# Twelve token tiles instead of eight gathered inside the expert loops, with eight x buffers instead of four

## The reference

```python
x = x + 0.5 * ffn(layernorm(x), ...)
x = x + attn(layernorm(x), ...)
x = x + 0.5 * ffn(layernorm(x), ...)

# ffn: 16 experts, top 4 per token, hidden width 176, and one shared expert
scores = sigmoid(logits) + gate_b
weights, indices = top_k(scores, 4); weights = weights / weights.sum(-1)
shared_out = silu(x @ w1_shared) * (x @ w3_shared) @ w2_shared
h3 = silu((x @ w1_routed[e]) * (x @ w3_routed[e]))
routed_out = sum over the 4 chosen e of weights[e] * (h3 @ w2_routed[e])
return shared_out + routed_out

# attn: xp = x W_in; dt = softplus(xp W_dt + b_dt); a = exp(-dt * exp(log_A))
# ys[t] = a[t] * ys[t-1] + xp[t]; y = ys W_out
```

## Time and profile before

| | |
|---|---|
| median of 3 runs | 588.59 us (586.60 to 590.25) |
| profiled execution | 588.09 us, span 586.1 us |
| mean granted TensorE clock | 0.912 |
| busy: PE, DVE, ACT, POOL | 83%, 75%, 64%, 60% of the span |
| x gathers (L562) | 158, 0.945 us each on POOL |
| early row gathers (L576) | 64, about 1.01 us each on POOL |
| late row gathers (L597) | 64, 0.978 us each on POOL |

### The profile page before, as it was taken

How to read it: one execution, slowest core, us unless ns; L and a number is a source line. 1 busy time by engine, 2 the same in 40 slices (tenths; PEclk the granted TensorE clock), 3 DMA queues, 4 the chain that set the end, 5 groups by cost and what they waited for, 6 DMA issues and landing times.

```text
span 586.1 us, 13303 instructions
## 1 busy us (share of the span) xinstructions
PE 486.1 (83%) x3206; PEld 448.6 (77%) x3207; DVE 437.3 (75%) x1467; ACT 372.2 (64%) x1128; POOL 353.3 (60%) x364
## 2 busy tenths in 40 slices
PE   3968789999999999687677942699999999998760
PEld 2856569999999999566565921499999999987650
DVE  6889838878888888638987589476778888867355
ACT  2687737777777777667675563477777777766100
POOL 3699754447777775477603252554467777755775
PEclk9989559999999999999997975599999999999975
DMA  8992044656656556443201460245455555674655
GB/s 283 394 350 91 27 136 109 170 163 201 200 163 169 162 165 151 132 122 107 72 2 55 144 215 1 63 115 158 135 160 159 160 173 159 157 153 136 193 165 152
DMA packets 61149, 88.25 MB, mean 151 GB/s; under 512 B 9499, under 2 KB 46363, under 8 KB 61107
## 3 DMA queue, kind: packets, MB, share of 16 engines
q0 software_dynamic: 13728, 37.50, 25.9%
q1 hardware_dynamic: 47379, 50.29, 25.0%
HBM read 57.22 MB, written 30.54 MB: 150 GB/s over the span
## 4 chain that ended last, share of the span: by engine, by line
PE 59%; DVE 12%; DMA 8%; ACT 8%; issue 6%; POOL 6%; SPq 0%; POOLq 0%; ACTq 0%; DVEq 0%
PE bank L1381 27%; PE bank L1432 13%; DMA ys_scratch<-ring_f 6%; PE bank L1402 5%; POOL mamba_room L597 5%; PE bank L1443 3%; PE bank L1442 3%; PE bank L1489 2%; PE bank L1600 1%; DVE lg L933 1%; ACT ring_f L691 1%; PE bank L1454 1%; DMA raw_shared<-in_w13s 1%; DVE stage L1012 1%; DVE ring_f L1083 1%
## 5 line engine op out<-in xcount | busy, mean ns | idle before, releaser
L562 POOL DMA_INDIRECT ring_f<-xn_scratch,tokidx x158 | 149.4, 945 | 110.5 <-PE bank L1402 65.5
L1432 PE MATMUL bank<-w_routed,ring_r 128*128 x790 | 120.3, 282 | 4.5 <-ACT ring_f L691 3.6
L1432 PEld LDWEIGHTS bank<-w_routed,ring_r 128*128 128x128 f32 x790 | 109.6, 188 | 6.6 <-issue 6.5
L674 ACT ACTIVATE ring_r<-bank 128x256 fp32r<-128x256 f32 x158 | 60.9, 385 | 64.5 <-PE bank L1443 62.3
L1381 PE MATMUL bank<-w_routed,ring_r 128*128 x480 | 99.7, 344 | 0.0
L1381 PE MATMUL bank<-w_routed,ring_x 128*128 x468 | 94.6, 337 | 0.0
L1381 PEld LDWEIGHTS bank<-w_routed,ring_r 128*128 128x128 f32 x480 | 78.2, 196 | 0.1
L597 POOL DMA_INDIRECT mamba_room<-ys_scratch,si x64 | 62.6, 978 | 19.5 <-issue 18.3
L961 DVE TENSOR_TENSOR ring_r<-bank,ring_r 128x128 fp32r<-128x128 f32 x158 | 45.9, 290 | 38.1 <-ACT ring_r L674 37.0
L1381 PEld LDWEIGHTS bank<-w_routed,ring_x 128*128 128x128 f32 x468 | 74.1, 190 | 0.0
L691 ACT ACTIVATE ring_f<-bank 128x256 f32<-128x256 f32 x158 | 60.6, 384 | 16.8 <-DMA ys_scratch<-ring_f 13.2
(11 more groups left out here) (185 smaller groups left out, 997.2 us busy)
## 6 DMA issues: line engine op xcount, KB each, us to landing
ys_scratch<-ring_f SPq DMA_DIRECT2D x158, 128.0 KB
raw_routed<-in_w13r SPq DMA_DIRECT2D x6, 704.0 KB, 12.4
xn_scratch<-w_routed SPq DMA_DIRECT2D x32, 128.0 KB, 4.4
raw_routed<-in_w2r SPq DMA_DIRECT2D x6, 512.0 KB, 12.7
...
ring_f<-xn_scratch,tokidx POOLq DMA_INDIRECT x158
...
```

Of the source, the lines that this page charges most:

```text
L562: pool.indirect_dma_start(xg[j % UN], None, xn_dram, bass.IndirectOffsetOnAxis(ap=tokidx[:, j:j + 1], axis=0)).then_inc(s_g[j % UN], 16)
L674: act.activation(hT[b][0], p_hT[b][:, 0:2 * P], ACT.Copy).then_inc(s_hhi, 1)
L1432: last = pe.matmul(p_y[b][:, 0:D], a, v, start=(q == 0), stop=(q == 4))
```

## The change

The room for gathered x grows from four to eight buffers: a new tile ring_g of 4 KB per partition, paid for by the descriptor scratch, which goes from 8192 to 4096 bytes per partition. An x gather now waits for the tile eight before. Twelve token tiles instead of eight (48 rows) are fetched early, from behind x gather 35, five rows to seven x gathers; the rows from n = 32 on follow the last x gather without a wait for y of their own, and their adds stand five to eight steps from step NS = 79 on. A row in the loop is added in the step of its own number instead of three later. Four token tiles (16 gathers) remain late, and their waits on marks of the scan layer and of the shared part are gone. Seven tiles are measured in DVE's loop, five behind it. The shared sums hang on tiles 12, 13 and 14.

```diff
-EARLY_TILES = 8
+EARLY_TILES = 12
 EARLY = EARLY_TILES * TOPK
 ROWS = 6
-EARLY_FIRST, EARLY_ADD = 31, 3
+XG = 8
+EARLY_FIRST, IN_LOOP = 35, 32
 LATE = NT - EARLY_TILES
-ROOMS = 6
+LATE_WHOLE = LATE - 2
-MEASURED = 5
-SCALED = ((0, 4), (4, EARLY_TILES))
+MEASURED = 7
+SCALED = ((0, 4), (4, 8), (8, EARLY_TILES))
-SUMS_AFTER = {9: (0, 1), 10: (2,), 11: (3,), 12: (4,), 13: (5,), 14: (6, 7)}
+SUMS_AFTER = {12: (0, 1), 13: (2, 3), 14: (4, 5, 6, 7)}
...
-        xg = [ring_f[:, k * D:(k + 1) * D] for k in range(UN)]
+        ring_g = sb("ring_g", [P, (XG - UN) * D])
+        xg = [ring_f[:, k * D:(k + 1) * D] for k in range(UN)] + [ring_g[:, k * D:(k + 1) * D] for k in range(XG - UN)]
...
         def early_after(n):
-            return max(4 * (n // TOPK) + EARLY_FIRST, EARLY_FIRST + 2 * n)
+            return max(4 * (n // TOPK) + EARLY_FIRST, EARLY_FIRST + 7 * n // 5)
         def early_step(n):
-            return early_after(n) + EARLY_ADD
+            return early_after(n) if n < IN_LOOP else NS + (n - IN_LOOP) * 5 // 8
...
             def gather(f, j):
-                if j >= UN:
-                    pool.wait_ge(s_xt, f * STEPS + NT + j - UN + 1)
+                if j >= XG:
+                    pool.wait_ge(s_xt, f * STEPS + NT + j - XG + 1)
...
             def fetch_early(f, n):
                 if n >= ROWS:
                     pool.wait_ge(s_ea, f * EARLY + n - ROWS + 1)
-                if early_after(n) >= NS:
-                    pool.wait_ge(s_y, f * NS + NS - EARLY + n - 1)
...
             def combine(f, t):
-                if f == 0:
-                    if k >= ROOMS:
-                        pool.wait_ge(s_cd, combined_to(f, t - ROOMS))
                 for q in range(TOPK):
-                    if f == 0 and q % 2 == 0 and 2 * k + q // 2 >= 1:
-                        reached, chunks = MAMBA_DONE[2 * k + q // 2 - 1]
-                        pool.wait_ge(m_s[reached], chunks)
-                    if f == 1 and q % 2 == 0 and 2 * k + q // 2 >= 1:
-                        done, pairs = SHARED_DONE[2 * k + q // 2 - 1]
-                        pool.wait_ge(s_st if done == "turned" else s_sy, pairs)
...
                     for t in range(MEASURED, EARLY_TILES):
                         last = measured(t)
                     link(last)
                     spread(1)
+                    spread(2)
...
-... dynamic_dma_scratch_size=8192)
+... dynamic_dma_scratch_size=4096)
```

49 lines of the change are left out of this document (23 added, 26 removed).

## The result

The changed kernel took 573.02 us (median of 4 runs, 572.31 to 574.64) against 589.42 us for the kernel before (4 runs, 586.60 to 591.62). The ratio on record is 0.9747, with a 95% interval of 0.9718 to 0.9776; it is not formed from the two medians, whose quotient is 0.9722. Forecast were 574.5 us, in a range of 569.5 to 584. All comparisons in this document are between executions in the chip's faster state: one of the kernel before (595.85 us) and one of pads_apart (825.35 us) were in the slower one and are left out. The profiled execution took 572.8 us, its span is 571.0 us, 15.1 us shorter than the one before.

A forecast was written before the change was run, and what follows sets the result against it. PE was taken to bound the loops, DVE the first tail and POOL's late gathers the second. 588.09 - 16.6 (second tail) + 1.5 (first tail) + 1.0 (writes) = 574.0; against the median, 574.5 us, range 569.5 to 584.

The forecast's parts named there:

- the second tail: End of layer 2: 16 fewer late gathers at POOL's pace, starting later; gain 16.6 us, bounds 14 and 20.3.
- the loops: Routed loops: denser gathers at 1.29 us against break-even 1.32, margin 2 us, so PE never waits for x.
- the first tail: After layer 1's loop: later spread(1) +2.8, slower matmuls +1.8, shorter Mamba steps -3.1; sum +1.5 us, between -3.1 and +5.
- The shared sums: Second tail: DVE's sums end at 565.2, before the last landing, cost nothing; if PE's clock stays low, 1 to 2 us lost.
- The rival in which the adds hold the gathers: Loops: each row add holds a gather for its whole 0.48 us, PE waits 10.5 us per loop; 595 us, chance 7%.
- The writes: Loops: denser gathers could make more steps slowed by y writes; +1.0 us for both loops, between 0 and 7.
- the rival in which the writes slow the loops: Loops: all 44 dense steps run at 2.28 us, 13 us lost per loop; 600 us, chance 4% in full.
- the case in which half the gain goes: Write stalls, low clock holding the shared sums, first tail 5 instead of 1.5: together 5 to 9 us, 580 to 584; chance 20%.
- Scratch and waits: Descriptor scratch 8192 to 4096 bytes: zero cost, upper end 3 us; the prediction gives the late gathers' removed waits no separate term.

The follow-up runs named there:

- pads_apart: Changed kernel with the empty slots' x gathers reading rows 0 to 127 instead of all row 0 (some tokens read wrongly); 571.73 us, ratio 0.9708.
- waits_back: Changed kernel with the waits of the late gathers on Mamba chunks and shared part put back; 572.14 us, ratio 0.9725.
- warm24: spread_ahead plus 24 unread PE transposes filling the idle gap behind the first layer's loop; 568.85 us, ratio 0.9674.
- spread_ahead: Changed kernel with tile 7 measured and spread(1) done before the early rows added after the first layer's loop; 571.66 us, ratio 0.9717.
- x4: Changed kernel with four x buffers instead of eight, the rest of the change kept; 586.13 us, ratio 0.9988 to the kernel before.
- first33: spread_ahead with the first early row at x gather 33 instead of 35, 33 rows beside the x gathers; 570.75 us, ratio 0.9711.
- pads_true: first33 with empty slots' x gathers spread over rows 1 to 128, every token's own index kept; 570.50 us, ratio 0.9699.
- buffers_alone: Kernel before with eight x buffers and the smaller descriptor scratch, no other part of the change; 590.90 us, ratio 1.0034.

## Why the prediction was right

The mechanism is the one forecast: the kernel's end was POOL's late gathers in the second tail, and sixteen of them moved to where POOL had time. That the total came within 1.5 us is in part luck. Between the two profiled executions 15.1 us went, where the terms added up to 14.1: the second tail brought 1.6 us less than forecast, the loops 2.2 us more and the first tail 0.4 us more.

**The second tail** was the term that counted: -16.6 forecast, -15.0 measured. Its mechanism stands: sixteen gathers fewer at POOL's pace, a later start, an end on the last landing. From gather 78 to the end of the span it is 50.2 us instead of 65.4. Three of its numbers were a little off, all to one side. The first late gather came at 545.02 (544.5), the sixteen are 1.30 apart and not 1.27, so that the last starts at 564.54 (563.6), and it lands after 3.71 us (3.24, as the one read before). The end at 571.0 instead of 569.5 is the sum of these: 0.5, 0.4 and 0.5.

**The shared sums** stayed covered as costed in this execution: the last one ended at 565.62 against 565.2. But pair 4 went at 555.01 and not 2.4 us sooner than before, at 552.8. I had counted one add behind tile 12's last landing; DVE waits for the whole tile, and all four adds follow, 2.05 us from 552.10. And the cover that I cost at nothing is not always there. In two of the other traces with this order the last add stood behind DVE's own work: in waits_back the sums ended at 570.72 and the last add came at 572.32, in warm24 at 562.12 and 563.71. Pair 4 had waited 3.88 and 4.57 us there, with the granted clock at 0.50 behind it. This is the loss of 1 to 2 us that I had named for a low clock; their second tails took 43.7 and 42.8 us, against 42.1 in the changed kernel.

**The first tail** was forecast at +1.5 as +2.8 and +1.8 less 3.1, and each piece is in the trace: ACT's root 2.6 us later (253.43 for 250.84), the next eight matmuls 3.68 for 1.99 us, and two steps of 6.91 and 6.78 for 8.56 and 8.23, 3.10 us. Measured +1.1. The wait before PE's second group was 2.76 us where I had some 3.5. spread_ahead and warm24 take the first two away. In the changed kernel the low clock under the second group does follow the wait for spread(1), as forecast: the granted clock had been back at 1.00 from 251.1 us and fell again at 254.5. But the wait is not the only way to it. In spread_ahead, without that wait, the clock that had fallen at 246.5 stayed low over both groups.

**The loops** cost nothing, as forecast, and x4 shows that this rests on the lead alone. I had the interval at 1.29 us and the margin at 2 us; measured are 1.266 and 4.59 us from issue to transposition instead of 3.74, which leaves 2.6 us (232.98 - 225.78 - 4.59). The two errors go against each other. PE did not wait before that transposition of x4, so 4.59 is an upper limit; in first33, where PE waits 0.29 us for gather 78, it comes 4.42 us after the gather's start, and the margin is 2.8 us. The time above 3.74 belongs in part to the one row that the last, empty tiles read: in pads_true, with the rows apart, the same transposition comes after 3.68 us and waits for nothing. The rival in which the adds hold the gathers (595 us) is refuted: of the first loop's 74 gathers 7 took more than 1.0 us, the longest 1.12, beside an add in five of every seven steps.

The traces also tell which. Seven gathers of the first loop started inside an add, six of the long ones and the one at 197.92, and each ended 0.82 us after the add's end (159 to 306 ns of the add were left, and they took 0.98 to 1.12 us); the seventh long one, at 143.31, started inside L1128, which has two SBUF inputs as well. In the 23 cases where the add started during a gather, the gather kept 0.94 to 0.95 us and the add its 0.47 to 0.48. The Trainium skill, SBUF — State Buffer, section "SBUF: two separate sides", has whichever of the two starts first hold the ports for the whole instruction, while the other blocks. The trace agrees where the DVE instruction was first, and disagrees where the gather was, since the add was not held. The prediction read this rule too widely: by it the gather at 196.91, which was first, would have kept its 0.95 anyway, and what speaks against the rule there is the add at 197.11 with its 0.47.

**The writes** were forecast at +1.0, and the loops came out 1.2 us shorter: in neither did denser gathers make more slow steps. Of the terms this one was wrong. That the loops really became shorter isn't shown, since identical loops differ by as much from one execution to the next; that the denser gathers cost nothing to be seen is shown. I had named the empty tiles' reads of one row beside the density of the gathers, and priced the density. In pads_apart, with the density unchanged, half of ACT's waits for writes went with the one row; and gathers of that kind are as many after as before. With this the rival in which the writes slow the loops (600 us) has lost its ground. Of the parts of the case in which half the gain goes, the stalls on writes did not come, and the low clock that holds the sums came only in the two traces named above.

**Scratch and waits**: no gain, as costed. For the waits, waits_back shows no difference; for the scratch, buffers_alone (1.0001 to 1.0066) leaves room for a cost of up to some 4 us, which isn't told apart from zero.
